# A triangular inverse on TensorE: the second of two matrices is turned on the chip at each level where a product made it before

## The chip, the cores and the metric

One core of one Trainium2 chip runs the whole program in one launch. The metric is the device time of that launch in microseconds (us).

## The reference

Two layers. The first is a recurrent one: for every token of two sequences of 4096 tokens a 512x512 state W and a bias b take one gradient step, and the token's output is read from the new state.

```python
def step(carry, kvq):
    W, b = carry
    k, v, q = kvq
    g = 2.0 / d_h * (W @ k + b - v)
    W = W - LR * jnp.outer(g, k)
    b = b - LR * g
    return ((W, b), W @ q + b)
```

The second is a mixture of experts with one shared expert and the two best of eight for each token. Each layer is followed by a residual sum and a layer norm.

## The kernel before

The recurrence is worked off in 32 steps of 128 tokens (`t` = 0 to 31), both sequences (`b` = 0 and 1) side by side. Within a step, the 128 dependent updates become one unit triangular system of 128x128 for each sequence. Its inverse is needed before the step's updates `U` can be formed (`u_part`), and those before the outputs and the new state.

The inverse is built in four stages. VectorE first inverts the eight diagonal blocks of 16x16 by substitution (`subst`, 30 small instructions). The rows of the blocks reach all partitions by one product with a mask (`spread_blocks`), whose moving operand `R` has 16 x 2 x 16 = 512 columns. Then three levels (`n` = 0, 1, 2) join blocks of 16, 32 and 64. The kernel keeps the matrix `M` (in `MM[:, 0]`) and its transpose (in `MM[:, 1]`). `inv_m` turns the transpose once on TensorE, and ScalarE copies the result to `MM[:, 0]`. A level is: `inv_t`, a product of the system's matrix `LT` with `M`; a masked copy to `T1` on VectorE; `inv_n`, products of `T1` with the transpose; and a subtraction from `MM` on VectorE. On levels 0 and 1, `inv_n` makes two products for each sequence, one for `M` and one for its transpose; on level 2 only the one for the transpose. These products are in plain float32, and each of them stands as two matmul instructions in the trace. All large products of the kernel are instead made of three instructions in float32r (`mm3`, lines 107 to 109), a high part and a low part of each operand.

Each engine follows a list written out by hand. TensorE's puts other work between the dependent parts of the inverse: halves of the next step's key projection (`k_proj`, six matmuls of 512 columns), halves of `qs_part` (six as well), and the shared expert of the step before. That expert's parts are `up_x1`, `back_x1` (two transposes), `down_x1` (six matmuls of 512 columns), once for each sequence. Its hidden tile `Hp1` (`HH` and `HL` in the trace) exists once: ScalarE writes `HH` for sequence 1 only after TensorE's `down_x1` of sequence 0 has read it. In `scalar_program`'s `back_x1` that is

```python
w.wait_ge(k.s_dn1, i)
w.wait_ge(k.s_HS1, i + 1)
copy(k.Hp1[0][:], at["HB", t, b][:, 0:H]).then_inc(k.s_HH1, 1)
```

After the 32 steps the experts of the second layer run over 149 tiles of gathered tokens, up to the end. Two groups of tokens are routed earlier: VectorE does this routing in between its other work, most of it in steps 14 and 26.

Of the kernel before, what the change touches and what calls it, by code (L numbers as in the profile page):

```python
# [15 lines left out]
P = 128  # L16
# [10 lines left out]
LEVELS = [16, 32, 64]  # L27
NL = len(LEVELS)
# [61 lines left out]
def groups_of(NT):  # L90
# [7 lines left out]
    return out, slot  # L98

# [150 lines left out]
def first_memory(k):  # L250

    nc, ctx = k.nc, ExitStack()
    with ctx:
# [30 lines left out]
        k.R = k.MM[:].rearrange("p k b n -> p (k b n)").rearrange("p (i b j) -> p i b j", i=BS, b=NB)  # L284
# [125 lines left out]
def tensor_program(k, e):  # L410
# [86 lines left out]
    def inv_n(t, n):  # L497
# [118 lines left out]
    for t in range(NT):  # L616
# [9 lines left out]
        inv_m(t)  # L626
        if more:
# [31 lines left out]
        else:  # L659
# [106 lines left out]
def scalar_program(k, e):  # L766
# [142 lines left out]
    for t in range(NT):  # L909
# [11 lines left out]
        inv_m(t)  # L921
# [112 lines left out]
def vector_program(k, e):  # L1034
# [39 lines left out]
    def scores(t):  # L1074
# [12 lines left out]
        rows = [P, BS, NB, BS]  # L1087
# [3 lines left out]
        tt(k.R, gd.unsqueeze(1).to_broadcast(rows), unit_lr.unsqueeze(2).unsqueeze(3).to_broadcast(rows), ALU.mult).then_inc(k.s_R, 1)  # L1091
# [944 lines left out]
```

## Time and profile before

| | us |
|---|---|
| median of 3 runs | 2392.36 (2389.82 to 2395.69) |
| the profiled execution, its own time | 2394.0 |
| its span in the trace | 2392.2 |
| TensorE busy with matmuls in the span | 2230.7 |
| VectorE busy | 1534.3 |
| ScalarE busy | 883.9 |

The span is what the trace covers, from the first instruction to the last; 1.8 us of the execution's own time lie around it. Busy times are sums over instructions, and matmuls overlap one another, so a busy TensorE says that it had work and not that it was at its peak. A start-to-start distance of matmuls is what one of them costs in a dense stream.

### The profile page before, as it was taken

What the parts mean: (1) busy time and instruction counts of PE and PEld (TensorE: products, weight loads), DVE (VectorE), ACT (ScalarE), POOL (GpSimd) and SP (SyncE); (2) the same over time, 40 slices, a digit from 0 to 9 for tenths busy, and PEclk for the clock granted to TensorE, in tenths of its full rate; (3) what the DMA queues carried; (4) which work ended last, traced back from release to release, by engine and by line L of the source; (5) the groups of instructions that cost most, each with busy time, mean ns of one, the idle gap of its engine ahead of it and who ended that gap; (6) DMA issues with size and microseconds to landing.
All of it is one profiled execution on the core that took longest, in us unless ns stands there. A gap on an engine that the chain in (4) does not pass through costs nothing.

```text
span 2392.2 us, 40085 instructions
## 1 busy us (share of the span) xinstructions
PE 2230.7 (93%) x13154; PEld 1939.7 (81%) x13154; DVE 1534.3 (64%) x3594; ACT 883.9 (37%) x1887; POOL 1113.8 (47%) x1061
## 2 busy tenths in 40 slices
PE   6999999999999999999999999999869999999860
PEld 5788888888888878888888887888759999989750
DVE  5655666655556667655556667665656545888886
ACT  3333333333333333333333333333346555555420
POOL 1233343433333334644445453356355453777776
PEclk9999999999999999999999999999979999999995
DMA  4011111111111111111111111111264455998996
GB/s 164 18 41 49 36 36 45 45 36 41 49 36 36 36 45 36 45 36 41 49 36 36 45 45 36 36 36 37 93 212 151 152 154 179 307 312 298 298 310 209
DMA packets 102486, 233.26 MB, mean 98 GB/s; under 512 B 18256, under 2 KB 18768, under 8 KB 101520
## 3 DMA queue, kind: packets, MB, share of 16 engines
q1 hardware_dynamic: 75744, 157.96, 18.5%
q0 software_dynamic: 26256, 72.71, 10.5%
q8 instruction: 113, 1.85, 0.3%
q14 instruction: 85, 0.70, 0.1%
q10 hardware_dynamic: 288, 0.04, 0.0%
HBM read 141.11 MB, written 89.53 MB: 96 GB/s over the span
## 4 chain that ended last, share of the span: by engine, by line
PE 82%; DVE 6%; POOL 4%; issue 4%; DMA 3%; ACT 1%; SPq 0%; DVEq 0%; POOLq 0%; ACTq 0%
PE banks L107 23%; PE banks L109 23%; PE banks L108 23%; PE banks L113 7%; POOL RG L1811 2%; PE banks L709 2%; DMA RG<-ys,POS 1%; PE banks L447 1%; PE banks L546 1%; PE banks L731 1%; POOL b_small L1683 1%; DMA ys<-b_Y 1%; POOL b_XN L1799 1%; DVE xc L1055 1%; DVE W L1052 1%
## 5 line engine op out<-in xcount | busy, mean ns | idle before, releaser
L107 PE MATMUL banks<-W 128*128 128x512 f32 (+1 forms) x2040 | 752.9, 369 | 15.9 <-DVE W L1052 15.9
L109 PE MATMUL banks<-W 128*128 128x512 f32 (+1 forms) x2040 | 717.8, 352 | 0.0
L108 PE MATMUL banks<-W 128*128 128x512 f32 (+1 forms) x2040 | 716.6, 351 | 0.0
L107 PEld LDWEIGHTS banks<-W 128*128 128x128 f32 x2040 | 388.5, 190 | 67.7 <-POOL W L1683 15.0
L109 PEld LDWEIGHTS banks<-W 128*128 128x128 f32 x2040 | 387.2, 190 | 54.0
L108 PEld LDWEIGHTS banks<-W 128*128 128x128 f32 x2040 | 388.7, 191 | 50.7 <-issue 7.2
L772 ACT ACTIVATE W<-banks 128x512 fp32r<-128x512 f32 x320 | 191.0, 597 | 521.3 <-DVE banks L1052 243.3
L1683 POOL TENSOR_TENSOR W<-S,W 128x512 fp32r<-128x512 f32 x256 | 327.8, 1306 | 117.3 <-ACT W L772 117.2
L1683 POOL TENSOR_TENSOR X<-X,B 128x1024 f32<-128x1024 f32 x32 | 78.8, 2464 | 620.6 <-DMA X<-in_x 620.6
L772 ACT ACTIVATE W<-S 128x512 fp32r<-128x512 f32 (+1 forms) x288 | 180.4, 650 | 227.8 <-DVE S L1052 211.8
L1052 DVE TENSOR_TENSOR W<-banks,W 128x512 fp32r<-128x512 f32 x192 | 132.2, 688 | 172.3 <-ACT W L772 172.3
L1799 POOL DMA_INDIRECT b_XN<-x1d,IDX x149 | 147.6, 991 | 137.3 <-PE banks L709 107.6
L107 PE MATMUL banks<-W,b_XL 128*128 x596 | 180.9, 304 | 2.0 <-DVE b_XL L1052 1.8
L1055 DVE SCALAR_TENSOR_TENSOR W<-banks,W 128x512 fp32r<-128x512 f32 x128 | 88.6, 692 | 134.1 <-ACT W L772 133.9
L109 PE MATMUL banks<-W,b_XH 128*128 x596 | 168.3, 282 | 0.0
L108 PE MATMUL banks<-W,b_XH 128*128 x596 | 168.0, 282 | 0.0
L1811 POOL DMA_INDIRECT RG<-ys,POS x128 | 139.2, 1087 | 42.2 <-issue 31.4
L1052 DVE TENSOR_TENSOR S<-S,banks 128x512 f32<-128x512 f32 x248 | 156.0, 678 | 0.2 <-issue 0.2
L107 PE MATMUL banks<-W,b_HL 128*128 x298 | 130.7, 439 | 23.0 <-DVE b_HL L1052 22.9
L1730 POOL DMA_INDIRECT ids<-idt,POS x128 | 126.0, 984 | 37.5 <-issue 37.5
L1052 DVE TENSOR_TENSOR b_HL<-banks,b_HH 128x256 fp32r<-128x256 f32 x149 | 62.6, 420 | 110.8 <-ACT b_HH L772 110.8
L772 ACT ACTIVATE b_XH<-banks 128x512 fp32r<-128x512 f32 x149 | 89.1, 598 | 119.3 <-PE banks L709 119.2
(156 smaller groups left out, 4433.6 us busy)
## 6 DMA issues: line engine op xcount, KB each, us to landing
ys<-b_Y SPq DMA_DIRECT2D x149, 256.0 KB
XT<-in_xT SPq DMA_DIRECT2D x32, 512.0 KB, 3.5
X<-in_x SPq DMA_DIRECT2D x32, 512.0 KB, 3.5
x1d<-X SPq DMA_DIRECT2D x64, 256.0 KB, 2.0
zd<-X SPq DMA_DIRECT2D x64, 256.0 KB, 2.0
b_Y<-zd SPq DMA_DIRECT2D x64, 256.0 KB, 5.1
out<-b_Y SPq DMA_DIRECT2D x64, 256.0 KB, 4.4
S<-in_we SPq DMA_DIRECT2D x32, 256.0 KB, 4.6
```

The lines of the kernel that those rows point to most:

```text
L107: e.matmul(o, ll, rh, start=start, stop=False, skip_group_check=True)
L108: e.matmul(o, lh, rl, start=False, stop=False, skip_group_check=True)
L109: return e.matmul(o, lh, rh, start=False, stop=stop, skip_group_check=True)
L113: return e.matmul(o, lhsT, rhs, start=start, stop=stop, skip_group_check=True)
L709: z = e.transpose(o[:, c], k.XN[i % XNS][:, c], ident)
L772: return e.activation(o, i, ACT.Copy, scale=scale)
L1052: return e.tensor_tensor(o, x, y, op)
L1055: return e.scalar_tensor_tensor(out=o, in0=x, scalar=s, in1=y, op0=op0, op1=op1)
L1683: return e.tensor_tensor(o, x, y, op)
L1730: e.indirect_dma_start(k.ids[g["x"]], off, k.idt[:, n:n + 1], None).then_inc(k.d_scatter.sem(m), 16)
L1799: e.indirect_dma_start(k.XN[i % XNS][:], None, k.x1d, off).then_inc(k.d_xs.sem(i), 16)
L1811: e.indirect_dma_start(k.G[j][c % 2], None, k.ys[f.g["x"]], off).then_inc(k.d_gather.sem(m), 16)
```

## The change

On every level the matrix is made by turning its transpose. `inv_m` takes the level `n` as well: TensorE turns `MM[:, 1]` before each of the three `inv_t`, ScalarE copies the result to `MM[:, 0]`, and `inv_t` waits for that copy. `inv_n` makes the product for the transpose alone on all levels, and VectorE's subtraction shrinks from 512 to 256 columns on levels 0 and 1. The order of the lists changes around it. The spread of the blocks leaves out what the substitution never reads: the first 8 rows of a block are sent whole, the last 8 with their last 8 columns only, which makes 8x2x16 + 8x2x8 = 384 columns of 512.

```diff
+HS = BS // 2
+BLK = NB * HS * (BS + HS)
+def block_rows(x):
+    n = NB * HS * BS
+    return [x[:, 0:n].rearrange("p (i b j) -> p i b j", i=HS, b=NB), x[:, n:BLK].rearrange("p (i b j) -> p i b j", i=HS, b=NB)]
 (tensor_program)
     def spread_blocks(t):
-        w.wait_ge(k.s_R, t + 1)
-        mm(e, o, k.cst[:, 2, :], k.R.rearrange("p i b j -> p (i b j)")).then_inc(k.s_Lb, 1)
+        w.wait_ge(k.s_R, 2 * t + 2)
+        mm(e, o[:, 0:BLK], k.cst[:, 2, :], k.R).then_inc(k.s_Lb, 1)
-    def inv_m(t):
-        w.wait_ge(k.s_M, NL * t + 1)
+    def inv_m(t, n):
+        w.wait_ge(k.s_M, NL * t + n + 1)
     def inv_t(t, n):
-        w.wait_ge(k.s_M0, t + 1)
-        w.wait_ge(k.s_M, NL * t + n + 1)
+        w.wait_ge(k.s_M0, NL * t + n + 1)
     def inv_n(t, n):
         for b in range(NB):
-            if not last:
-                mm(e, o[:, b * P:(b + 1) * P], k.MM[:, 1, b, :], k.T1[:, b, :])
-            z = mm(e, o[:, (2 + b) * P:(3 + b) * P], k.T1[:, b, :], k.MM[:, 1, b, :])
+            z = mm(e, o[:, b * P:(b + 1) * P], k.T1[:, b, :], k.MM[:, 1, b, :])
 (the order of a step, TensorE)
             qs_part(t, 0, 0)
-            inv_t(t, 1)
+            inv_m(t, 1)
             if t > 0:
                 down_x1(t - 1, 0)
-            else:
-                qs_part(t, 0, 1)
+            inv_t(t, 1)
+            qs_part(t, 0, 1)
             inv_n(t, 1)
-            if t > 0:
-                qs_part(t, 0, 1)
             k_turn(n, 0)
             k_proj(n, 1, 0)
-            inv_t(t, 2)
+            inv_m(t, 2)
             if t > 0:
                 down_x1(t - 1, 1)
-            else:
-                k_proj(n, 1, 1)
+            inv_t(t, 2)
+            k_proj(n, 1, 1)
             inv_n(t, 2)
-            if t > 0:
-                k_proj(n, 1, 1)
 (the order of the last step, TensorE)
             down_x1(t - 1, 0)
+            inv_m(t, 1)
+            down_x1(t - 1, 1)
             inv_t(t, 1)
-            down_x1(t - 1, 1)
+            qs_part(t, 1, 0)
             inv_n(t, 1)
-            qs_part(t, 1, 0)
+            qs_part(t, 1, 1)
+            inv_m(t, 2)
             inv_t(t, 2)
-            qs_part(t, 1, 1)
             inv_n(t, 2)
 (scalar_program)
-    def inv_m(t):
-        w.wait_ge(k.s_MM, t + 1)
-        w.wait_ge(k.s_T, NL * t)
+    def inv_m(t, n):
+        w.wait_ge(k.s_MM, NL * t + n + 1)
+        w.wait_ge(k.s_T, NL * t + n)
         if t > 0:
             back_x1(t - 1, 1)
+        inv_m(t, 1)
         if more:
             k_turn(n, 0)
             next(soft_steps, None)
+            inv_m(t, 2)
             k_proj(n, 1)
 (vector_program)
-        if n < NL - 1:
-            mmv = k.MM[:].rearrange("p k b n -> p (k b n)")
-            tt(mmv, mmv, o, ALU.subtract).then_inc(k.s_M, 1)
-            return
-        tt(mt, mt, o[:, 256:512], ALU.subtract).then_inc(k.s_MT, 1)
+        tt(mt, mt, o[:, 0:256], ALU.subtract).then_inc(k.s_MT if n == NL - 1 else k.s_M, 1)
             k_proj(n, 0)
-            inv_t(t, 1)
             if t > 0:
                 back_x1(t - 1, 1)
                 down_x1(t - 1, 0)
+            inv_t(t, 1)
             inv_n(t, 1)
             k_turn(n, 0)
-            inv_t(t, 2)
             if t > 0:
                 down_x1(t - 1, 1)
+            inv_t(t, 2)
             inv_n(t, 2)
 (vector_program, scores)
-        tt(k.R, gd.unsqueeze(1).to_broadcast(rows), unit_lr.unsqueeze(2).unsqueeze(3).to_broadcast(rows), ALU.mult).then_inc(k.s_R, 1)
+        for h, o in enumerate(block_rows(k.R)):
+            rows = [P, HS, NB, (BS, HS)[h]]
+            own = unit_lr[:, h * HS:(h + 1) * HS].unsqueeze(2).unsqueeze(3)
+            tt(o, gd[:, :, h * HS:BS].unsqueeze(1).to_broadcast(rows), own.to_broadcast(rows), ALU.mult).then_inc(k.s_R, 1)
```

TensorE, before, in the middle of step 1: level 1 from its first product to its last. `MM,LT` is `inv_t`, `WS,HL` and `WS,HH` are `down_x1` of sequence 0, `T,MM` is `inv_n`'s product for `M` and `MM,T` the one for its transpose. A row is one matmul call.

```order
L113 MATMUL banks<-MM,LT 128x128 [waits s_M,s_LGc]
L113 MATMUL banks<-MM,LT 128x128
L107 MATMUL banks<-WS,HL 128x512
L108 MATMUL banks<-WS,HH 128x512
L109 MATMUL banks<-WS,HH 128x512
L107 MATMUL banks<-WS,HL 128x512
L108 MATMUL banks<-WS,HH 128x512
L109 MATMUL banks<-WS,HH 128x512
L113 MATMUL banks<-T,MM 128x128 [waits s_T1,s_Klo]
L113 MATMUL banks<-MM,T 128x128
L113 MATMUL banks<-T,MM 128x128
L113 MATMUL banks<-MM,T 128x128
```

TensorE, after, the same place; `ident,MM` is the added turn, and the `banks<-W` at the end begin `qs_part`.

```order
L493 MATMUL banks<-ident,MM 128x128 [waits s_M,s_LGc]
L493 MATMUL banks<-ident,MM 128x128
L115 MATMUL banks<-WS,HL 128x512
L116 MATMUL banks<-WS,HH 128x512
L117 MATMUL banks<-WS,HH 128x512
L115 MATMUL banks<-WS,HL 128x512
L116 MATMUL banks<-WS,HH 128x512
L117 MATMUL banks<-WS,HH 128x512
L121 MATMUL banks<-MM,LT 128x128 [waits s_M0,s_Klo]
L121 MATMUL banks<-MM,LT 128x128
L115 MATMUL banks<-W 128x512
L116 MATMUL banks<-W 128x512
```

`inv_t` has moved from ahead of `down_x1` to right behind it, the turn stands where it was, and `inv_t` now waits for `s_M0`, ScalarE's copy.

ScalarE, before, in step 1, from the second activation of the shared expert on (`HH` is its copy for sequence 1):

```order
L851 ACTIVATE banks<-banks,small 128x128 [waits s_hb1]
L851 ACTIVATE banks<-banks,small 128x128
L772 ACTIVATE HH<-banks 128x256 [waits s_HS1,s_dn1]
L772 ACTIVATE W<-banks 128x4x128 [waits s_A,s_Pm,s_KT]
L772 ACTIVATE Kf<-banks 128x512 [waits s_K]
```

ScalarE, after, the same place:

```order
L854 ACTIVATE banks<-banks,small 128x128 [waits s_hb1]
L854 ACTIVATE banks<-banks,small 128x128
L775 ACTIVATE HH<-banks 128x256 [waits s_HS1,s_dn1]
L775 ACTIVATE MM<-banks 128x256 [waits s_T,s_MM]
L775 ACTIVATE W<-banks 128x4x128 [waits s_A,s_Pm,s_KT]
L775 ACTIVATE MM<-banks 128x256 [waits s_T,s_MM]
L775 ACTIVATE Kf<-banks 128x512 [waits s_K]
```

The copy of level 1 stands directly behind the copy to `HH`, which waits for `s_dn1`; the copy of level 2 stands between the copies of the turned and the projected keys.

## Rows read from the trace of the kernel before

**Rows 1.** The page: busy time by engine, and the chain that ended last.

```profile
PE 2230.7 (93%) x13154; PEld 1939.7 (81%) x13154; DVE 1534.3 (64%) x3594; ACT 883.9 (37%) x1887; POOL 1113.8 (47%) x1061
PE 82%; DVE 6%; POOL 4%; issue 4%; DMA 3%; ACT 1%; SPq 0%; DVEq 0%; POOLq 0%; ACTq 0%
```

**Rows 2.** Busy time in stretches: two plain steps, then step 14, which has routing.

```profile
core 0: us, PE busy (x) PEld busy (x) DVE busy (x) ACT busy (x) POOL busy (x), PEclk, DMA share, GB/s
691.00:743.60 52.60, 52.58 (x302) 45.45 (x301) 31.95 (x83) 17.39 (x35) 18.98 (x16) 1.00 0.12 41
744.00:796.00 52.00, 51.98 (x296) 44.88 (x296) 31.39 (x83) 16.92 (x33) 18.98 (x16) 1.00 0.12 41
796.20:856.70 60.50, 54.75 (x303) 46.15 (x302) 43.79 (x106) 21.62 (x39) 20.13 (x16) 0.98 0.10 36
```

**Rows 3.** Timeline of level 1 in step 12: start, duration, engine, instruction.

```profile
696.62 0.40 PE L109 MATMUL banks<-W 128*128 128x512 f32 x1
696.86 0.61 PE L113 MATMUL banks<-MM,LT 128*128 128x128 f32 x4
697.53 0.39 PE L108 MATMUL banks<-WS,HH 128*128 128x512 f32 x1
...
698.46 0.40 PE L109 MATMUL banks<-WS,HH 128*128 128x512 f32 x1
...
698.89 0.39 ACT L772 ACTIVATE HH<-banks 128x256 fp32r<-128x256 f32 x1 [2.62 <-PE banks L109]
...
699.65 0.68 DVE L1052 TENSOR_TENSOR X<-banks,X 128x512 f32<-128x512 f32 x1
699.82 0.39 PE L108 MATMUL banks<-W 128*128 128x512 f32 x1
700.04 0.39 PE L109 MATMUL banks<-W 128*128 128x512 f32 x1
...
700.74 0.40 PE L109 MATMUL banks<-W 128*128 128x512 f32 x1
700.98 0.60 PE L447 MATMUL banks<-ident,Kf 128*128 128x128 f32 x4
701.65 0.39 PE L108 MATMUL banks<-W 128*128 128x512 f32 x1
```

**Rows 4.** Timeline of TensorE around one spread of the blocks (`MM,cst`).

```profile
733.39 1.02 PE L113 MATMUL banks<-MM,cst 128*128 128x512 f32 x2
734.48 0.39 PE L108 MATMUL banks<-W 128*128 128x512 f32 x1
```

**Rows 5.** Instructions of tile HH, and what its engine waited for.

```profile
L772 ACT ACTIVATE HH<-banks x64: 383/385/386, 112.2 to 1758.4; 128x256 fp32r<-128x256 f32 x64
...
  PE banks L109: 81.2, 31
```

**Rows 6.** Timeline of ScalarE at the one copy to `MM` of step 12.

```profile
691.42 0.38 ACT L772 ACTIVATE HF<-banks 128x256 f32<-128x256 f32 x1
691.69 0.39 ACT L772 ACTIVATE MM<-banks 128x256 f32<-128x256 f32 x1
```

**Rows 7.** Timeline of step 0: the one place where `inv_t` waited for that copy.

```profile
55.12 0.38 ACT L772 ACTIVATE MM<-banks 128x256 f32<-128x256 f32 x1
...
55.65 0.68 PE L113 MATMUL banks<-MM,LT 128*128 128x128 f32 x4 [0.30 <-ACT MM L772]
...
56.40 0.40 PE L108 MATMUL banks<-W 128*128 128x512 f32 x1
```

**Rows 8.** Subtraction from `MM`, by shape: total busy us, mean ns.

```profile
L1052 DVE TENSOR_TENSOR MM<-MM,banks 128x512 f32<-128x512 f32 x64 | 43.7, 683 | 58.9 <-PE banks L113 58.9
L1052 DVE TENSOR_TENSOR MM<-MM,banks 128x256 f32<-128x256 f32 x32 | 13.2, 412 | 2.2 <-PE banks L113 2.2
```

**Rows 9.** Stretches with an idle TensorE near step 15; columns as in rows 2.

```profile
843.40:845.90 2.50, 0.35 (x2) 0.00 (x0) 2.50 (x5) 0.54 (x2) 2.50 (x3) 1.00 0.00 0
851.50:854.10 2.60, 0.00 (x0) 0.00 (x0) 2.56 (x12) 0.00 (x0) 0.00 (x0) 1.00 0.00 0
854.40:857.80 3.40, 3.40 (x16) 3.31 (x16) 1.04 (x3) 2.93 (x6) 0.00 (x0) 0.52 0.00 0
908.60:909.90 1.30, 0.02 (x1) 0.05 (x1) 1.30 (x6) 0.00 (x0) 0.00 (x0) 1.00 0.00 0
```

More of the change, by code:

```diff
@@ L283, in first_memory @@
         k.onesr, k.cst = sb("onesr", [P], F32R), sb("cst", [NCST, P])
-        k.R = k.MM[:].rearrange("p k b n -> p (k b n)").rearrange("p (i b j) -> p i b j", i=BS, b=NB)
+        k.R = k.MM[:].rearrange("p k b n -> p (k b n)")[:, 0:BLK]
         k.xc, k.rw = sb("xc", [NB, BS]), sb("rw", [KC, E])
@@ L476, in spread_blocks @@
         o = bank(w, ("Lb", t), k.s_sub, 2 * (BS - 1) * (t + 1))
-        w.wait_ge(k.s_R, t + 1)
-        mm(e, o, k.cst[:, 2, :], k.R.rearrange("p i b j -> p (i b j)")).then_inc(k.s_Lb, 1)
-    def inv_m(t):
-        o = bank(w, ("MM", t), k.s_M0, t + 1)
-        w.wait_ge(k.s_M, NL * t + 1)
+        w.wait_ge(k.s_R, 2 * t + 2)
+        mm(e, o[:, 0:BLK], k.cst[:, 2, :], k.R).then_inc(k.s_Lb, 1)
+    def inv_m(t, n):
+        o = bank(w, ("MM", t, n), k.s_M0, NL * t + n + 1)
+        w.wait_ge(k.s_M, NL * t + n + 1)
         for b in range(NB):
@@ L625, in tensor_program @@
             up_x1(t - 1, 1)
-        inv_m(t)
+        inv_m(t, 0)
         if more:
@@ L808, in scores @@
         copy(k.ATp[0][:], kq).then_inc(k.s_AThi, 1)
-    def inv_m(t):
-        w.wait_ge(k.s_MM, t + 1)
-        w.wait_ge(k.s_T, NL * t)
-        copy(k.MM[:, 0, :, :].rearrange("p b n -> p (b n)"), at["MM", t][:, 0:256]).then_inc(k.s_M0, 1)
+    def inv_m(t, n):
+        w.wait_ge(k.s_MM, NL * t + n + 1)
+        w.wait_ge(k.s_T, NL * t + n)
+        copy(k.MM[:, 0, :, :].rearrange("p b n -> p (b n)"), at["MM", t, n][:, 0:256]).then_inc(k.s_M0, 1)
     def inv_end(t):
@@ L920, in scalar_program @@
             up_x1(t - 1, 1)
-        inv_m(t)
+        inv_m(t, 0)
         if more:
@@ L935, in scalar_program @@
                 split_w(m)
+            inv_m(t, 2)
         inv_end(t)
@@ L1086, in scores @@
         e.tensor_reduce(gd, k.T1[:].rearrange("p b (k j) -> p b j k", k=NBL), AX.X, ALU.add).then_inc(k.s_sc, 1)
-        rows = [P, BS, NB, BS]
         w.wait_ge(k.s_sc, 4 * t + 3)
@@ L1090, in scores @@
         w.wait_ge(k.s_MTlo, t)
-        tt(k.R, gd.unsqueeze(1).to_broadcast(rows), unit_lr.unsqueeze(2).unsqueeze(3).to_broadcast(rows), ALU.mult).then_inc(k.s_R, 1)
-        w.wait_ge(k.s_R, t + 1)
+        for h, o in enumerate(block_rows(k.R)):
+            rows = [P, HS, NB, (BS, HS)[h]]
+            own = unit_lr[:, h * HS:(h + 1) * HS].unsqueeze(2).unsqueeze(3)
+            tt(o, gd[:, :, h * HS:BS].unsqueeze(1).to_broadcast(rows), own.to_broadcast(rows), ALU.mult).then_inc(k.s_R, 1)
+        w.wait_ge(k.s_R, 2 * t + 2)
         stt(kq, kq, -1.0, mAT.unsqueeze(1).to_broadcast(bc), ALU.add, ALU.mult).then_inc(k.s_sc, 1)
@@ L1099, in subst @@
     def subst(t):
-        n0, lb = 2 * (BS - 1) * t, at["Lb", t].rearrange("p (i b j) -> p i b j", i=BS, b=NB)
+        n0, (upper, lower) = 2 * (BS - 1) * t, block_rows(at["Lb", t])
         w.wait_ge(k.s_Lb, t + 1)
@@ L1105, in subst @@
         for b in range(NB):
-            stt(k.xc[:, b, 1:BS], lb[:, 0, b, 1:BS], unit[:, 0:1], unit[:, 1:BS], ALU.mult, ALU.add).then_inc(k.s_sub, 1)
+            stt(k.xc[:, b, 1:BS], upper[:, 0, b, 1:BS], unit[:, 0:1], unit[:, 1:BS], ALU.mult, ALU.add).then_inc(k.s_sub, 1)
         yield
@@ L1111, in subst @@
                 w.wait_ge(k.s_sub, n0 + 2 * j + b - 1)
-                stt(rest, lb[:, j, b, j + 1:BS], k.xc[:, b, j:j + 1], rest, ALU.mult, ALU.add).then_inc(k.s_sub, 1)
+                row = upper[:, j, b, j + 1:BS] if j < HS else lower[:, j - HS, b, j + 1 - HS:HS]
+                stt(rest, row, k.xc[:, b, j:j + 1], rest, ALU.mult, ALU.add).then_inc(k.s_sub, 1)
             yield
@@ L1488, in vector_program @@
             tick()
-            inv_t(t, 1)
-            tick()
             if t > 0:
@@ L1495, in vector_program @@
                 tick()
+            inv_t(t, 1)
+            tick()
             inv_n(t, 1)
@@ L1499, in vector_program @@
             tick()
-            inv_t(t, 2)
-            tick()
             if t > 0:
@@ L1504, in vector_program @@
                 tick()
+            inv_t(t, 2)
+            tick()
             inv_n(t, 2)
@@ L1519, in vector_program @@
             down_x1(t - 1, 0)
-            inv_t(t, 1)
             split_w(1)
             down_x1(t - 1, 1)
+            inv_t(t, 1)
             inv_n(t, 1)
@@ L1525, in vector_program @@
             inv_t(t, 2)
+            inv_n(t, 2)
             split_w(4)
-            inv_n(t, 2)
             split_w(6)
```

## The prediction

> **What bounds the kernel now.** I read the page first: TensorE is busy for 2230.7 us of 2392.2, and the chain that ended last runs on it for 82% [rows 1]. Then the stretches, since an average mixes 32 steps with the experts behind them. In a plain step TensorE is busy 52.58 of 52.60 us, at full granted clock, with VectorE at 31.95 and ScalarE at 17.39 us [rows 2]. So in these steps every matmul taken away is time taken away, and every wait of TensorE's is time added, in full: there is no idle time in the step for a new wait to hide in. Steps 14 and 26 (60.50 us for the first of them [rows 2]) have some on TensorE, where VectorE's routing is late. Last I read one step's timeline for what a matmul costs in the stream [rows 3] and for what ScalarE is doing when it will be wanted [rows 3, 5].
>
> **What the change removes.** Take the distance from a 512-column matmul, over a small group and one L107, to the next L108. Over `inv_t`'s four instructions it is 697.53 - 696.62 = 0.91 us; over `inv_n`'s eight it is 699.82 - 698.46 = 1.36 us [rows 3]. The difference, 0.45 us, is four instructions, which is exactly what a level loses. Levels 0 and 1 each lose it: 0.90 us a step.
>
> **What it adds on TensorE.** Four transposes, two each ahead of levels 1 and 2. The group of four key transposes takes 701.65 - 700.74 = 0.91 us by the same measure [rows 3]; two 512-column matmuls are in it, at 0.23 each (four of them from 699.82 to 700.74), so four transposes cost 0.91 - 0.46 = 0.45 us, the price of two products. A transpose is one instruction where a product is two, and they cost the same each. Bounds: 0.42 to 0.46.
>
> **The spread.** From its start to the next L108 are 734.48 - 733.39 = 1.09 us, 0.23 of which is the L107 between: 0.86 us for 512 columns [rows 4]. With 384 columns three quarters: 0.215 us less. TensorE is dense there, so it counts. If a fixed part does not shrink, it is a little less; lower bound 0.15.
>
> So TensorE's own work shrinks by 0.90 - 0.45 + 0.215 = **0.665 us a step**, 20.6 us over steps 0 to 30.
>
> The Trainium skill ("Perfetto Trace Analysis", Transposes) asks that a logical transpose be made by the transpose and not by a standard matmul, and gives as its reason that arithmetic is skipped. By that rule the change is right as it stands; the rows agree only on the count of instructions, since one transpose instruction costs the 0.11 us that one pass of a product costs.
>
> **What it adds as a wait.** `inv_t` of a level now waits for ScalarE's copy to `MM`. What is queued ahead of that copy on ScalarE decides. On level 0 nothing changes. On level 1 the copy stands directly behind `back_x1` of sequence 1, whose last instruction, the copy to `HH`, waits for `down_x1` of sequence 0. The trace shows this wait in every step: ScalarE idles 2.62 us and starts 0.43 us after the start of `down_x1`'s last matmul [rows 3], 31 times [rows 5]. It hurt nobody. But in the new order TensorE runs turn, `down_x1` of sequence 0, `inv_t`. So `down_x1`, meant as the cover for the copy, is what the copy waits for, through the ScalarE queue: the cover is gone entirely. Counted from the start of that last matmul:
>
> - `HH` starts at 0.43;
> - the next ScalarE instruction starts 0.27 later, as 691.42 to 691.69 for a copy of the same size followed by this very copy [rows 6]: 0.70;
> - the copy to `MM` takes 0.39 [rows 6]: 1.09;
> - TensorE starts `inv_t` 0.15 after the copy's end (55.12 + 0.38 to 55.65), and from there to the next L108 are 56.40 - 55.65 = 0.75 [rows 7]: 1.99.
>
> Without a wait the same distance is 0.91 [rows 3], 0.23 of it for the first matmul; the restart alone costs 0.75 - 0.68 = 0.07. The wait costs **1.08 us**, in each of steps 1 to 30. Bounds: 0.9 if part of the restart is an artefact of modelled matmul ends; 1.3 if the copy's reads and ScalarE's waits add one more handover of 0.15 to 0.2.
>
> Who else is late? VectorE's masked copy to `T1` on level 1 now stands behind `HL` and the residual sum of `down_x1`. The sum starts at 1.19 after my zero and takes 0.68 [rows 3]; `inv_t` ends near 1.24 + 0.68 = 1.92, so `T1` is done near 2.4, and `inv_n` comes at 1.24 + 0.44 + 6 x 0.23 = 3.06. Covered by 0.6 us. On level 2 the copy is behind the copy of the turned keys, whose transposes are a half `k_proj` (1.4 us) older, and a whole `down_x1` of 1.4 us lies between turn and `inv_t`, against 0.04 + 0.39 + 0.15 = 0.58 of need. Covered. In step 14 the routing's exponential sits between, still covered by my count, by about 0.1 us.
>
> **The ends.** In step 0 there is no shared expert, so on levels 1 and 2 `inv_t` follows its turn at once. A group of four transposes lasts 0.60 and its last starts at 3 x 0.11 [rows 3], so the last ends 0.27 after its start; 0.04 + 0.39 + 0.15 bring `inv_t` to 0.85 instead of 0.11, and the restart costs 0.07 more: 0.8 us each, 1.6 together, less 0.665. That is +0.9. In the last step level 2 has nothing between turn, `inv_t` and `inv_n`: two bare handovers of about 0.8, less 0.665, less 0.27 for level 0's subtraction, for which level 1 waits there and which takes 412 ns in place of 683 [rows 8]. I take +0.7 (0 to 2). In steps 14 and 26 TensorE waits for VectorE near the step's end anyway (2.5 us with 0.35 busy [rows 9]), so the spread's 0.215 is not gained there: +0.4. The first spread, in the prologue, is on the way: -0.2.
>
> **Sum.** 30 x (1.08 - 0.665) = +12.5; +0.9 + 0.7 + 0.4 - 0.2 = +1.8. Together +14.3 us. Against the profiled execution's own 2394.0 that is 2408.3; that execution stands 1.6 above the median of the runs, 2392.4, from which the forecast is 2406.7, say **2406.5 us**. A difference of 0.3%, 7.2 us, is about what a measurement of this kernel can tell from no change.
>
> **Rivals.**
>
> *The copy is hidden* (7%). If ScalarE's copy to `MM` did not have to stand behind `HH`, or `HH` were released early, only the savings stay: -20.6 + 1.8 = -18.8, or 2373.6 us. This is the case on the other side; it decides as soon as the wait costs less than 0.665 us a step. Against it stands the 2.62 us idle of ScalarE in [rows 3] and the order of its instructions.
>
> The Trainium skill ("PSUM — Partial Sum Buffer", Engine vs sequencer instructions) says that ScalarE's queue is strictly first in, first out, while TensorE may pull a weight load ahead but keeps its matmuls in order. By that rule nothing overtakes `HH`, and the forecast stands; the 2.62 us of idle agree, for the copy of the turned keys behind it had nothing to do with `down_x1`.
>
> *The wait is there but smaller* (5%). With 0.6 to 0.9 us a step the result lies between -0.2 and +9: 2392 to 2401, mostly within 0.3%. For it: the ends of matmuls are modelled. Against it: `HH` starts at a fixed 0.43 us behind, so the real end is where it is modelled.
>
> *The clock falls* (4%). After 2.60 us of an idle TensorE the granted clock was 0.52 for 3.40 us [rows 9], the lower level of 1.2 GHz in place of 2.4; at half speed such a stretch loses 1.7 us. If each new wait brought that, 30 x 1.7 = 51 us come on top: 2458. Against it: after 1.3 us idle at 908.6, longer than the new wait, and during the 2.5 us at 843.4 the clock stayed at 1.00 [rows 9].
>
> The Trainium skill ("TensorE: Matmul & The Clock Gate", Part 4: PE-mode transpose) says that transposes do not count as work for the clock, which would favour this rival since the change adds some. No row here shows it: plain steps, which hold such groups as the one at 700.98 [rows 3], run at 1.00 [rows 2].
>
> *VectorE becomes the one waited for* (within the forecast's range). If the 0.6 us of cover for `T1` were gone, each step would lose up to 0.3 us more, 9 us in all: 2416.
>
> **How the numbers follow.** The forecast has 84%. Its own spread comes from 0.9 to 1.3 us for the wait (-5 to +7), the spread product (2 us), the ends (1 us) and the runs' own scatter (3 us); the two low terms rarely meet, so I give 2400 to 2413 for eight in ten. Slower by over 0.3%: 0.88, which takes in the clock's rival and the forecast. Faster: 0.07. Within: 0.05.
>
> **What would show it.** In a plain step of the changed kernel: `inv_t` of level 1 with an idle time ahead of it near 0.8 us, put down to ScalarE's `MM`; `HH` still with its 2.6 us idle, and an `MM` copy 0.27 us behind it; no idle ahead of `inv_t` of level 2; plain steps longer by 0.4 us, each with eight instructions of the `inv_n` kind gone and four transposes come. Wrong if the copy on ScalarE starts before `HH`, if TensorE waits at another place, or if the clock in the plain steps is under 1.00.

## The result, and the profile after

The changed kernel takes 2415.41 us, the median of 4 runs (2412.13 to 2419.0), against 2392.69 for the kernel before beside it: 1.0092 times as long [1.008, 1.0104], 22.7 us more. The forecast was 2406.5 us with a range of 2400 to 2413, so the sign is right and the size is not. The profiled execution took 2416.47 us, span 2414.7.

The page of the changed kernel, busy time by engine (compare [rows 1]):

```profile
PE 2225.8 (92%) x13026; PEld 1927.7 (80%) x13026; DVE 1526.3 (63%) x3626; ACT 901.8 (37%) x1951; POOL 1113.5 (46%) x1061
```

TensorE is busy for 4.9 us less, with 128 instructions fewer, and yet the span is 22.5 us longer: the change saved work and added waiting. (The busy time is a sum over overlapping rows and holds the half-clock stretches; what was saved in a step is measured below.) Where, is asked of the waits first. The two largest of TensorE's waits between step 1 and the last step, in the changed kernel (engine, line, releaser; total us, times, longest):

```profile
PE banks L121 <- ACT MM L775: 27.3, 32, 1.1
PE banks L115 <- DVE X1l L1058: 12.0, 6, 2.7
```

The same question to the kernel before:

```profile
PE banks L107 <- DVE X1l L1052: 12.5, 6, 2.7
PE banks L113 <- ACT MM L772: 1.1, 1, 1.1
```

The waits for `X1l` stand still, 12.5 us before and 12.0 after. Those for `MM` have gone from one to 32, from 1.1 to 27.3 us. Thirty of them are level 1 of steps 1 to 30, 0.84 us each; the other two are at level 0, in steps 1 and 27. `L121` is `inv_t`'s product, `ACT MM` the copy of the turned matrix. One of these waits, level 1 of step 12, in the timeline of the changed kernel (start, duration, engine, instruction; in brackets the idle time before it and what ended it); it answers to [rows 3]:

```profile
700.93 0.38 PE L493 MATMUL banks<-ident,MM 128*128 128x128 f32 x2
...
702.30 0.40 PE L117 MATMUL banks<-WS,HH 128*128 128x512 f32 x1
702.74 0.38 ACT L775 ACTIVATE HH<-banks 128x256 fp32r<-128x256 f32 x1 [2.09 <-PE banks L117]
703.02 0.38 ACT L775 ACTIVATE MM<-banks 128x256 f32<-128x256 f32 x1
703.15 0.42 DVE L1058 TENSOR_TENSOR HL<-banks,HH 128x256 fp32r<-128x256 f32 x1 [2.26 <-ACT HH L775]
703.50 0.68 DVE L1058 TENSOR_TENSOR X<-banks,X 128x512 f32<-128x512 f32 x1
...
703.54 0.68 PE L121 MATMUL banks<-MM,LT 128*128 128x128 f32 x4 [0.84 <-ACT MM L775]
...
704.29 0.39 PE L116 MATMUL banks<-W 128*128 128x512 f32 x1
```

Read from the top. `down_x1`'s last matmul starts at 702.30. ScalarE, idle for 2.09 us (the prediction's sign said 2.6), is released by it and copies `HH` at 702.74. Only then, 0.28 us later, does it copy `MM`, whose transposes, at 700.93, were done long before. TensorE stands idle for 0.84 us and restarts at 703.54. From 702.30 to the next L116 at 704.29 are 1.99 us, the figure that the prediction had added up. A whole plain step, from its first turn to the next one's (columns as in [rows 2]):

```profile
695.40:748.50 53.10, 52.24 (x298) 44.95 (x297) 31.60 (x84) 18.02 (x37) 19.02 (x16) 1.00 0.12 41
```

53.10 us, where the kernel before has 52.65 by the same measure (the starts of the first `ident,MM` of one step and the next; most plain steps repeat it within 0.05). The granted clock stays at 1.00, its upper level, so the idle 0.84 us costs no clock. The spread and the turns, by shape, in the changed kernel (total us, mean ns of one, idle before):

```profile
L493 PE MATMUL banks<-ident,MM 128*128 128x128 f32 x192 | 36.7, 272 | 3.8 <-DVE MM L1058 3.8
...
L121 PE MATMUL banks<-MM,cst 128*128 128x384 f32 x64 | 26.1, 488 | 0.3 <-DVE S L1058 0.2
```

Stage by stage, in the two profiled executions. Each stage is bounded by starts on TensorE: the first turn of a step, the first matmul of `u_part` in the last step, the first transpose of the experts.

| stage | before, us | after, us | difference | forecast |
|---|---|---|---|---|
| prologue, to step 0's first turn | 53.5 | 51.9 | -1.6 | -0.2 |
| step 0 | 56.91 | 58.17 | +1.3 | +0.9 |
| steps 1 to 30 | 1600.0 | 1613.7 | +13.7 | +12.9 |
| last step, to `u_part` | 15.92 | 20.51 | **+4.6** | +0.7 |
| `u_part` to the experts | 38.30 | 38.83 | +0.5 | 0 |
| experts | 627.5 | 631.5 | +4.1 | 0 |

Steps 1 to 30 came out as forecast. The last step did not, and neither did the experts, which are looked at further down. The first two rows can't be read from one pair of traces: the prologue of the kernel before took 51.8 us in its later trace and 53.5 here, and step 0 varies with the clock. Step 0 of the changed kernel took 58.17 us at a mean granted clock of 0.91 and 55.67 at 1.00 (`after_again` below, the same program); at 0.94 the changed levels took 57.64 (`hh_again` below) and the old ones 56.9 and 57.2 (the two traces of the kernel before), which makes +0.4 to +0.7.

The end of the last step in the changed kernel, where the inverse's result `MTl` is due at TensorE:

```profile
1738.99 0.42 DVE L1058 TENSOR_TENSOR MM<-MM,banks 128x256 f32<-128x256 f32 x1 [0.80 <-PE banks L121]
1739.33 3.43 DVE L1058 TENSOR_TENSOR W<-S,W 128x512 fp32r<-128x512 f32 x2
1739.34 2.86 POOL L1688 TENSOR_TENSOR X<-X,B 128x1024 f32<-128x1024 f32 x1 [18.73 <-DMA X<-in_x]
...
1742.17 3.12 POOL L1688 TENSOR_TENSOR W<-S,W 128x512 fp32r<-128x512 f32 x2
1742.68 1.48 DVE L1058 TENSOR_TENSOR MTl<-MM,MTh 128x256 fp32r<-128x256 f32 x1
...
1744.30 0.77 PE L115 MATMUL banks<-W,MTl 128*128 128x512 f32 x1 [5.36 <-DVE MTl L1058]
```

The same place in the kernel before:

```profile
1724.84 0.42 DVE L1052 TENSOR_TENSOR MM<-MM,banks 128x256 f32<-128x256 f32 x1 [0.81 <-PE banks L113]
1725.18 0.68 DVE L1052 TENSOR_TENSOR W<-S,W 128x512 fp32r<-128x512 f32 x1
...
1725.81 0.43 DVE L1052 TENSOR_TENSOR MTl<-MM,MTh 128x256 fp32r<-128x256 f32 x1
...
1726.38 0.47 PE L107 MATMUL banks<-W,MTl 128*128 128x512 f32 x1 [1.58 <-DVE MTl L1052]
...
1726.67 2.41 POOL L1683 TENSOR_TENSOR X<-X,B 128x1024 f32<-128x1024 f32 x1 [19.36 <-DMA X<-in_x]
```

Before, between `MM` and `MTl` on VectorE stands one split of an expert weight (`W<-S,W`), 0.68 us, and TensorE waits 1.58 us. Only after `MTl` does GpSimd start its 128x1024 sum `X<-X,B`. In the changed kernel two splits stand there, for the change also moves `inv_n` of level 2 in VectorE's list for the last step, a part of the edit that the excerpt of the change does not show:

```diff
 (vector_program, the order of the last step)
             inv_t(t, 2)
+            inv_n(t, 2)
             split_w(4)
-            inv_n(t, 2)
             split_w(6)
             inv_end(t)
```

The two splits take 3.43 us in place of two times 0.68: one by one 0.68 and 2.83. `MTl` takes 1.48 in place of 0.43. TensorE waits 5.36 us. All the while GpSimd is at work: on that sum, which starts within 0.01 us of the splits, and from 1742.17 on splits of its own. That is two theories at once: the order of the list (O), and a VectorE that slows beside GpSimd (G).

### The profile page after: what moved, and what is told of

Its sections match the earlier page's. It is cut to its first block, busy times and chain, and to the rows that moved or that the text cites. A ratio compares the mean times of both kernels' runs of the same rounds, so it can differ in the third digit from the quotient of the medians.

```text
span 2414.7 us, 39989 instructions
## 1 busy us (share of the span) xinstructions
PE 2225.8 (92%) x13026; PEld 1927.7 (80%) x13026; DVE 1526.3 (63%) x3626; ACT 901.8 (37%) x1951; POOL 1113.5 (46%) x1061
## 4 chain that ended last, share of the span: by engine, by line
PE 81%; DVE 6%; issue 4%; POOL 4%; DMA 3%; ACT 1%; SPq 0%; DVEq 0%; POOLq 0%; ACTq 0%
PE banks L115 23%; PE banks L117 23%; PE banks L116 23%; PE banks L121 6%; PE banks L712 2%; POOL RG L1816 2%; DMA RG<-ys,POS 2%; PE banks L455 1%; PE banks L551 1%; PE banks L734 1%; PE banks L493 1%; DVE xc L1061 1%; POOL b_small L1688 1%; POOL b_XN L1804 1%; DVE W L1058 1%
## 5 line engine op out<-in xcount | busy, mean ns | idle before, releaser
L116 PE MATMUL banks<-W 128*128 128x512 f32 (+1 forms) x2040 | 717.3, 352 | 0.0
L116 PEld LDWEIGHTS banks<-W 128*128 128x128 f32 x2040 | 388.8, 191 | 46.5
L116 PE MATMUL banks<-W,b_XH 128*128 x596 | 169.4, 284 | 0.0
```

The costliest lines, as they stand in the source:

```text
L116: e.matmul(o, lh, rl, start=False, stop=False, skip_group_check=True)
```

## The experiments

The first four kernels below shared their runs of the kernel before, 2393.35 us (20 runs), which agrees with the 2392.69 of the result, so that they are compared with the changed kernel's 2415.41 too. In the later sessions every version, the kernel before included, took some 40 us longer, so that ratios are taken within a session only; what that was is looked at behind the last experiment. HH stands for the theory that `HH` ahead of the copy on ScalarE costs the step 1.08 us, O and G for the two above.

**Copy `MM` first.** The changed kernel, with ScalarE's copy for level 1 ahead of the copy to `HH`, in steps 1 to 30.

```diff
 (ScalarE, the copy to HH, sequence b of step t)
+        if b == 1 and t + 2 < NT:
+            inv_m(t + 1, 1)
         w.wait_ge(k.s_dn1, i)
         ...
         copy(k.Hp1[0][:], at["HB", t, b][:, 0:H]).then_inc(k.s_HH1, 1)
 (ScalarE, the order of a step)
             back_x1(t - 1, 1)
-        inv_m(t, 1)
+        if t == 0 or not more:
+            inv_m(t, 1)
```

> The changed kernel, with one move on ScalarE in steps 1 to 30: the copy to MM of level 1 stands ahead of the copy to HH (which waits for down_x1 of sequence 0), and no longer behind it. Theory A (the copy was late because it was queued behind HH): the idle time of 0.84 us ahead of inv_t of level 1 goes, a plain step falls from 53.10 us by 1.08 to 52.02, and the whole by 30 x 1.08 = 32.4 us, to about 2383 us, some 9.5 us under the kernel before. Rival B (the wait is the bare way from turn to copy to inv_t, and the queue has nothing to do with it): the step stays at 53.1 and the time at 2415 us. In between: what is left of the idle is the part that the queue does not explain.

Measured: 2390.13 us (10 runs), 0.9992 [0.9982, 1.0002] of the kernel before, and 25 us less than the changed kernel. The plain step is 52.31, not 52.02. So HH is right that the wait hangs on the queue, and 0.28 us a step remain. Level 1 of step 11 in this kernel:

```profile
637.85 0.39 ACT L775 ACTIVATE MM<-banks 128x256 f32<-128x256 f32 x1 [0.69 <-PE banks L493]
...
639.04 0.60 PE L121 MATMUL banks<-MM,LT 128*128 128x128 f32 x4
639.24 0.38 ACT L775 ACTIVATE HH<-banks 128x256 fp32r<-128x256 f32 x1 [1.01 <-PE banks L117]
...
639.65 0.42 DVE L1061 TENSOR_TENSOR HL<-banks,HH 128x256 fp32r<-128x256 f32 x1 [2.26 <-ACT HH L775]
...
640.00 0.68 DVE L1061 TENSOR_TENSOR X<-banks,X 128x512 f32<-128x512 f32 x1
...
640.59 0.41 DVE L1061 TENSOR_TENSOR T<-banks,smallc 128x256 f32<-128x256 f32 x1
640.64 0.40 PE L117 MATMUL banks<-W 128*128 128x512 f32 x1
...
641.06 0.52 PEld L121 LDWEIGHTS banks<-MM,T 128*128 128x128 f32 x4 [0.46 <-DVE T L1061]
641.06 0.71 PE L121 MATMUL banks<-MM,T 128*128 128x128 f32 x4
```

`MM` is now copied at 637.85 and `inv_t` starts at 639.04 with no wait. But `HH` still waits for `down_x1`, VectorE's `HL` and residual sum `X` for `HH`, and the masked copy to `T1` (`T<-banks`) stands behind both, at 640.59. `inv_n` waits for it: its weight load says 0.46 us. The row of the matmul itself shows no wait, because the modelled end of the matmul at 640.64 covers it; in a dense stream the next one would have started 0.23 behind, at 640.87, and it starts at 641.06, 0.19 late; its four instructions then take 0.71 us in place of 0.61. The two make the 0.28 us, within rounding. The prediction had given `T1` 0.6 us of cover. That cover was there only because `inv_t`, and `inv_n` behind it, were themselves 1.08 us late.

**A second buffer for `HH`.** The changed kernel; sequence 1's `HH` gets a tile of its own, so that its copy no longer waits for `down_x1` of sequence 0.

```diff
+        k.HH1s = [k.Hp1[0], sb("HH1b", [H], F32R)]
 (ScalarE)
-        w.wait_ge(k.s_dn1, i)
+        w.wait_ge(k.s_dn1, i - 1)
-        copy(k.Hp1[0][:], at["HB", t, b][:, 0:H]).then_inc(k.s_HH1, 1)
+        copy(k.HH1s[b][:], at["HB", t, b][:, 0:H]).then_inc(k.s_HH1, 1)
 (TensorE's down_x1 and VectorE's back_x1)
-        hi, lo = k.Hp1
+        hi, lo = k.HH1s[b], k.Hp1[1]
```

> The changed kernel with its lists as they are, and a second buffer for HH of sequence 1, so that this copy no longer waits for down_x1 of sequence 0. HL keeps its one buffer. Theory A: ScalarE's queue is free, the copy to MM follows the turn at once, the idle ahead of inv_t of level 1 goes, plain steps of about 52.02 us, the whole about 2383 us (-32), as with the copy moved ahead. Rival B: 2415 us, as nothing that stands between turn and inv_t has changed but the wait of another instruction. Rival C (it is the order of the lists, not the wait on the buffer, that costs): a remainder of 0.3 us or more per step.

Measured: 2380.29 us (4 runs), 0.9944 [0.9929, 0.9959]. The plain step is 52.03. TensorE's waits for `MM` between step 1 and the last step, in this kernel (both are at level 0), and then its level 1 of step 12:

```profile
PE banks L121 <- ACT MM L776: 1.8, 2, 0.9
```

```profile
686.45 0.38 ACT L776 ACTIVATE HH1b<-banks 128x256 fp32r<-128x256 f32 x1
...
687.04 0.38 ACT L776 ACTIVATE MM<-banks 128x256 f32<-128x256 f32 x1 [0.21 <-PE banks L494]
...
688.24 0.61 PE L121 MATMUL banks<-MM,LT 128*128 128x128 f32 x4
688.51 0.42 DVE L1059 TENSOR_TENSOR HL<-banks,HH1b 128x256 fp32r<-128x256 f32 x1 [1.91 <-PE banks L117]
...
689.45 0.41 DVE L1059 TENSOR_TENSOR T<-banks,smallc 128x256 f32<-128x256 f32 x1
...
690.08 0.61 PE L121 MATMUL banks<-MM,T 128*128 128x128 f32 x4
```

The `MM` copy follows its turn at 687.04, 1.2 us before `inv_t` starts, and `T1` is 0.2 us early instead of late. Only in steps 16 and 28 does TensorE wait for `T1` (0.55 and 0.42 us). 53.10 - 52.03 = 1.07 us a step is the price of the wait; the forecast said 1.08. With the queue released the change is worth having.

**The spread alone.** The kernel before, with the 384-column spread and nothing of the inverse.

```diff
+HS = BS // 2
+BLK = NB * HS * (BS + HS)
-        w.wait_ge(k.s_R, t + 1)
-        mm(e, o, k.cst[:, 2, :], k.R.rearrange("p i b j -> p (i b j)")).then_inc(k.s_Lb, 1)
+        w.wait_ge(k.s_R, 2 * t + 2)
+        mm(e, o[:, 0:BLK], k.cst[:, 2, :], k.R).then_inc(k.s_Lb, 1)
 (VectorE: k.R written in two parts, the rows of a block read from them, as in the change)
```

> The kernel before with the narrow spread alone (384 columns of 512, and its two VectorE instructions). Theory A's sum has 0.215 us a step for it: plain steps of 52.65 - 0.215 = 52.43 us, 31 x 0.215 = 6.7 us in all, 2386 us. Rival F (the two instructions on VectorE or the substitution behind them take it back, since VectorE had only 0.54 us to spare before the sum with B): plain steps between 52.5 and 52.65, and no difference that can be measured.

Measured: 2386.72 us (10 runs), 0.9972 [0.9962, 0.9981]; plain step 52.44. The spread gives 0.21 us a step, as forecast (0.215). What is left between 52.44 and 52.03 is the levels' own part: 0.41 us, where the forecast had 0.45.

**The splits behind `MTl`.** The changed kernel; in the last step VectorE makes `MTl` before the two splits. This takes theory O alone.

```diff
             inv_n(t, 2)
+            inv_end(t)
             split_w(4)
             split_w(6)
-            inv_end(t)
             split_w(7)
```

> The changed kernel with one move on VectorE in the last step alone: the low parts of weights 4 and 6 are made behind the low part of the inverse (MTl), not ahead of it. In the changed kernel they stood ahead of it for 3.4 us and TensorE idled 5.36 us before u_part. Theory D (this queue is the part that my sum of the ends left out): the idle before u_part falls to about 1.6 us, u_part comes 3.8 us earlier, and the time falls to about 2411.6 us. Rival E (the weights' transfers set the end of that phase anyway): u_part comes earlier, but the first expert tile at the same time as before, and the time stays at 2415 us.

Measured: 2411.35 us (4 runs), 1.0077 [1.0062, 1.0093]: 4.1 less than the changed kernel. The last step up to `u_part` is 18.25 us in place of 20.51, with TensorE still idle for 3.10, not 1.6:

```profile
1737.53 2.34 POOL L1688 TENSOR_TENSOR X<-X,B 128x1024 f32<-128x1024 f32 x1 [18.66 <-DMA X<-in_x]
...
1738.21 1.94 DVE L1058 TENSOR_TENSOR MTl<-MM,MTh 128x256 fp32r<-128x256 f32 x1 [0.55 <-ACT MTh L775]
...
1740.30 0.77 PE L115 MATMUL banks<-W,MTl 128*128 128x512 f32 x1 [3.10 <-DVE MTl L1058]
```

Nothing but `MTl` itself is left on VectorE here, and it takes 1.94 us for what takes 0.43 elsewhere. GpSimd's sum runs from 1737.53 to 1739.87. Moving the splits gives back 2.3 us, and what remains looks like G.

**GpSimd later.** To hold G against O, the changed kernel with its two splits ahead of `MTl`, but GpSimd's sum of the last step held back until `MTl` is made.

```diff
 (GpSimd)
         w.wait_ge(k.s_B, 2 * t)
+        if t == NT - 1:
+            w.wait_ge(k.s_MTlo, NT)
         tt(k.X[:], k.X[:], k.B[:], ALU.add).then_inc(k.s_XB, 1)
```

> The changed kernel with one more wait on GpSimd in the last step: its sum X + B starts only when VectorE has finished the low part of the inverse (MTl). Lists and work are the same. In the changed kernel this sum ran from 1739.34 to 1742.20 us, and two splits of weights and MTl on VectorE, which took 0.68, 0.68 and 0.43 us where GpSimd was idle, took 3.43 us for the two and 1.48 us in that stretch; with the splits moved behind, MTl took 1.94 us instead. Theory G (VectorE is slowed by GpSimd's large operation at the same time, and this is most of what the last step lost): the two splits and MTl take about 1.8 us together, the idle before u_part falls from 5.36 to about 2.2 us, the time by 3.2 us to about 2412 us. Rival H (the VectorE instructions are late or long for another reason, such as the transfers that land then): they stay long and the time stays at 2415 us.

Measured: 2454.79 us (7 runs) against 2436.69 for the kernel before beside it, in the second session, and the step up to `u_part` is 17.29 us. The changed kernel was not timed beside these two. The ratio, 1.0068 [1.0049, 1.0087], stands against its 1.0092 [1.008, 1.0104] in the first and 1.0097 [1.0075, 1.012] in the third; the intervals overlap, and the trace decides:

```profile
1759.38 1.29 DVE L1058 TENSOR_TENSOR W<-S,W 128x512 fp32r<-128x512 f32 x2
...
1760.58 0.42 DVE L1058 TENSOR_TENSOR MTl<-MM,MTh 128x256 fp32r<-128x256 f32 x1
...
1761.15 0.47 PE L115 MATMUL banks<-W,MTl 128*128 128x512 f32 x1 [2.14 <-DVE MTl L1058]
1761.17 2.67 POOL L1688 TENSOR_TENSOR X<-X,B 128x1024 f32<-128x1024 f32 x1 [20.47 <-DVE MTl L1058]
```

The same two splits take 1.29 us in place of 3.43, and `MTl` 0.42 in place of 1.48, with the same instructions, order and operands; only GpSimd is silent. That is 2.14 + 1.06 = 3.2 us, and the stage is 20.51 - 17.29 = 3.2 shorter. G is shown. The 2.14 us that TensorE still waits are 0.56 more than the 1.58 before: the second split, which is O by itself.

The rows say more than "slower". In `split_last` the sum ends at 1739.87 and `MTl` at 1740.15, 0.28 us behind it. Over the fourteen traces of this case, each of the 11 `MTl` that start while GpSimd is in such a sum or split ends 0.28 or 0.29 us behind GpSimd's end, and each of VectorE's 105 splits of 128x512 that do so ends 0.54 to 0.56 us behind, whether it lasts 1.03 us or 2.87. So VectorE's instruction waits until GpSimd's is done. The other way round it is GpSimd that gives way: in the changed kernel VectorE's first split starts 0.01 us ahead of the sum and takes its usual 0.68 us, and the sum takes 2.86 us where it took 2.34 in `split_last`. Work with an operand in PSUM does not wait. Two rows of the kernel before, from where GpSimd is in its sum and then in a split:

```profile
1727.99 1.40 DVE L1055 SCALAR_TENSOR_TENSOR W<-banks,W 128x512 fp32r<-128x512 f32 x2 [1.15 <-ACT W L772]
1729.31 1.57 DVE L1052 TENSOR_TENSOR W<-S,W 128x512 fp32r<-128x512 f32 x1
```

The two of the first row take 0.69 us each, as anywhere; the one of the second, with both operands in SBUF, takes 1.57 in place of 0.68.

**Both mends.** The second buffer and the splits behind `MTl` (`hh_and_split`), and with GpSimd held as well (`all_three`); the edits are the ones above.

> The changed kernel with the second buffer for HH and with the two splits of the last step moved behind MTl. If the two causes add up: 2380.3 (second buffer alone) less 2.3 us (what u_part gained in the trace with the splits moved, 20.51 to 18.25 us from the step's first turn) to less 4.1 us (what the whole gained): 2376 to 2378 us. Rival: the last step's gain is lost in the loading of weights behind it, 2380 us.

> The changed kernel with the second buffer for HH, the splits moved behind MTl and GpSimd's sum X + B held back until MTl is done. Theory G: MTl takes 0.43 us and not 1.9, u_part comes 16.6 to 17 us after the last step's first turn (15.9 before the change, 20.5 after it, 18.3 with the splits moved alone), and the time is 1 to 2 us under the run without the wait on GpSimd: 2375 to 2377 us, or 0.7% under the kernel before. Rival: holding GpSimd back delays the sum that o_part needs and gives it back, no difference to the run without it.

Measured: 2427.03 us (10 runs), 0.9964 [0.9946, 0.9982], and 2429.97 us (12 runs), 0.9968 [0.9955, 0.9981]. Holding GpSimd brings the stage before `u_part` from 17.81 to 16.39 us, but the whole gets nothing. The last step of `all_three`:

```profile
1731.05 5.13 DVE L1059 TENSOR_TENSOR W<-S,W 128x512 fp32r<-128x512 f32 x3
...
1731.31 2.66 POOL L1689 TENSOR_TENSOR X<-X,B 128x1024 f32<-128x1024 f32 x1 [19.60 <-DVE MTl L1059]
...
1736.84 0.50 PE L115 MATMUL banks<-W,ATl 128*128 128x512 f32 x1 [2.66 <-DVE W L1062]
```

The collision has only moved: now three splits meet GpSimd's sum and its own splits and take 5.13 us, and TensorE waits 2.66 us for VectorE at `ATl`. From `u_part` to the experts it is 40.63 us, where `hh_and_split` has 39.70.

**The same again, against each other.** A third session, with the changed kernel, the second buffer, both mends, and all three.

> The changed kernel itself once more, beside the three versions below on one chip. The last three runs were on another chip, where the kernel before took 2436.7 us in place of 2393.4 and the steps with scatters were longer in all versions, so their differences to runs of the first chip can't be read. Expected: 1.009 times the kernel before; in steps 1 to 13 53.10 us each; from the last step's first turn to u_part 20 to 21 us.

> The second buffer for HH alone, as in second_hh. Expected 0.9944 of the kernel before, steps 1 to 13 52.03 us, and 20 to 21 us from the last step's first turn to u_part.

> The second buffer for HH and the splits of the last step behind MTl. On the other chip 0.9964 of the kernel before there, 17.8 us from the last step's first turn to u_part. If the causes add up: 2.5 to 4 us under the second buffer alone, 0.9930 of the kernel before. If the loading of the weights behind the last step sets the time: no difference to the second buffer alone.

> The same and GpSimd's sum X + B held back until MTl is done. On the other chip u_part came 16.4 us after the last step's first turn, MTl took 0.43 us, but the next low part of u_part came late, behind three splits of weights that now met GpSimd's sum for 5.13 us. Theory G with that: u_part 1.4 us earlier than in the run before this one, o_part not earlier, and no difference in time between the two, within 2 us.

| kernel | us | ratio to before [95%] | plain step | last step, to `u_part` |
|---|---|---|---|---|
| changed | 2458.63 | 1.0097 [1.0075, 1.012] | 53.10 | 21.60 |
| second buffer | 2425.78 | 0.9972 [0.9961, 0.9984] | 52.00 | 20.92 |
| and splits behind `MTl` | 2421.42 | 0.9956 [0.994, 0.9972] | 52.00 | 17.75 |
| and GpSimd held | 2420.72 | 0.9949 [0.9934, 0.9964] | 52.00 | 16.41 |

The changed kernel's ratio repeats (1.0092, 1.0097). The last two rows can't be told apart. Both mends together beat the kernel before by 0.4%, and by their medians they are 4.4 us below the second buffer alone; the intervals of these two just overlap.

**What differs between the sessions.** The kernel before, unchanged, once more.

> The kernel before once more, for its trace in a session in which it takes about 2435 us and not 2393. If the session or chip costs every version the same: plain steps 1 to 13 of 52.65 us as in the first trace, steps 18 to 25 longer by 0.6 to 1 us each, the last two steps of the recurrence and the expert phase longer by 8 to 10 and by 20 to 25 us. If this chip is as fast as the first, the trace repeats the first one and says nothing on that.

Measured: 2435.14 us (8 runs), 1.0001 [0.9981, 1.0022] of itself. Its plain steps outside a few are 52.65, as in the first session. Longer are steps 18 to 25 (53.25 to 53.49), steps 29 and 30 (59.51 and 61.35), and the experts (648.0 in place of 627.5). So the extra 40 us lie in a few steps (20) and in the experts (20), and the plain steps and `u_part`'s stage (15.93) can be compared over all sessions. It weakens the comparison of whole times: the two mends' 0.4% holds in that condition; in the first session only the second buffer alone was timed, and was 0.56% faster, where the third gave it 0.28%. That it was another chip, as some of the expectations say, is not shown: the first and the third session are on record under the same chip number.

## Why the prediction was right in part

**Right, row for row: the wait at level 1.** `HH` behind `down_x1`, the copy 0.28 us behind `HH`, TensorE's restart, 1.99 us in all. Taking the queue's wait away brought 1.07 us a step (forecast 1.08). The spread brought 0.21 (0.215), the levels 0.41 (0.45). A plain step got 0.45 us longer (forecast 0.415). The wait and the spread are each shown by a run in which it alone was changed; the levels' part is what is left over.

ScalarE's copies come strictly in the order of the list: the `MM` copy's transposes start at 700.93 and end by 701.31 in the changed kernel's trace, and the copy starts at 703.02, behind `HH`. The Trainium skill ("PSUM — Partial Sum Buffer", Engine vs sequencer instructions) gives that as the rule, and by that rule the forecast of the sign held.

**Right in sum, not in place: steps 14, 15, 26, 27.** The forecast had 1.2 us for 14 and 26 together and 0.8 for 15 and 27. The traces give -0.07, +1.27, +0.05, +0.77, 2.0 us together as well. The shift between the two steps of a pair is one of the clock. Behind one of TensorE's idle times in a routing step (2.4 to 2.75 us) the granted clock is at its lower level for 3.4 us. In the kernel before, that stretch lies mostly in step 14 ([rows 9], 854.40 to 857.80; step 14 ends at 856.67). In the changed kernel it lies mostly in step 15, which begins at 861.99:

```profile
861.40:864.70 3.30, 3.30 (x12) 2.82 (x12) 1.20 (x3) 2.78 (x6) 0.00 (x0) 0.50 0.00 0
```

By half of the 1.5 us that changed sides, step 14 is shorter and step 15 longer by some 0.75 us (an estimate). In steps 26 and 27 it has moved the other way, and there TensorE's second wait for VectorE is 1.45 us in place of 2.74. So the sum of 2.0 is right by some luck.

**The step that failed: "In the last step level 2 has nothing between turn, `inv_t` and `inv_n` ... I take +0.7 (0 to 2)".** It was +4.6. The part that this sentence costed, the bare handovers, is about right. With the splits and GpSimd out of the way the stage is 16.4 us; 0.35 us of that is a gain of the second buffer, which these versions have too (TensorE waits 1.00 us ahead of level 1's turn, and 1.35 without the buffer). That leaves 16.75 against 15.92, +0.8. What the sentence left out is who else is on VectorE. The change also moves `inv_n` of level 2 ahead of `split_w(4)` in VectorE's list, so two splits stand between the last subtraction and `MTl`, where one stood. With GpSimd held back that costs 17.29 - 16.75 = 0.5 us, the 0.56 seen above. And that lands the splits and `MTl` beside GpSimd's sum and splits. The sum began 0.4 us behind `MTl`'s end before; the overlap costs 3.2 us. Together 0.8 + 0.5 + 3.2 = 4.5 of the 4.6 us. I had read the edit as a matter of TensorE's order, and counted only TensorE's instructions and ScalarE's copy in it. This step alone does not carry the time out of the range: with +4.6 in its place the sum gives 2410.6 us. The other 4 to 5 us are mostly the experts, which the sum had at nothing.

**A smaller miss: the 0.6 us of cover for `T1`.** It was right as a number and wrong as a reserve. It would have been gone as soon as the wait ahead of it was, and `copy_first` ran into that: the rival "The copy is hidden" priced at 2373.6 was 2390.13 for the one version and 2380.29 for the other. In the second, 0.04 us a step, the last step's 4.3 (20.93 - 15.92 - 0.7) and 1.6 for steps 16 and 28, which wait for `T1`, account for the 6.7 us that are missing.

**What is not explained.** Of the 22.5 us between the two spans the stages up to the experts give 18.4. The other 4.1 are the experts', whose code the change doesn't touch. Over the first session's traces this stage takes 627.5 and 625.8 us in the two versions with the old levels (the kernel before and `spread_only`) and 628.9 to 631.5 in the four with the changed ones, so a part of it may come from the change after all; by one trace each that is not shown. The changed kernel's trace has half-clock stretches in it where the kernel before has none, as here (columns as in [rows 2]):

```profile
1790.00:1793.40 3.40, 3.40 (x19) 3.40 (x18) 0.00 (x0) 0.90 (x2) 1.58 (x3) 0.53 0.72 212
```

They don't settle it: over the stage the mean granted clock is 0.94 before and 0.93 in the changed kernel, and 0.93 too in `spread_only`, the shortest of all. Why they come and go is open.

**The rivals.** "The clock falls" is refuted: 30 idle stretches of 0.84 us, and the granted clock is 1.00 in the plain steps. It fell behind a longer one: during the last step's idle 5.36 us it went to 0.50, and `u_part`'s first matmul takes 0.77 us in place of 0.47. "VectorE becomes the one waited for" is refuted for the changed kernel as it is, where `T1` appears among the waits only in the last step (0.52 us, one of the bare handovers), and true of `copy_first`. That this rival's 2416 us is so near the 2415.41 measured is chance; it also lay outside the range that it was said to be within.

## What to carry to other kernels

When a value now goes round by another engine, look at what is queued ahead of it there, and what *that* waits for. A cover that consists of the very work the queue waits for is none. Reorder the queue or, better, give the instruction ahead of it a buffer of its own: moving the copy left the next victim one step behind, and the buffer cured both in the plain steps.

Read a change of order on every engine's list, the last iteration's own list too. Ask of each engine what then runs at the same time: a slack found while another wait is in place is not a reserve, and a VectorE time taken beside a silent GpSimd doesn't hold beside a busy one. What it costs is the rest of GpSimd's instruction, so look for the longest one.

## What the runs showed of the hardware

- A VectorE subtraction of two SBUF tiles that starts while GpSimd is in its fp32 sum of 128x1024 or a split of 128x512 ends 0.28 us (128x256) or 0.55 us (128x512) behind GpSimd's instruction: up to 1.94 us in place of 0.42, and up to 2.87 in place of 0.68. With one operand in PSUM it takes its usual 0.69. The Trainium skill ("Perfetto Trace Analysis", Optimizing Scalar/DVE Operations) says that the two share an SBUF port; this case's rows agree, and put the price at the time that GpSimd's instruction has left. Whether it is that port was not tried by itself.
- An fp32 transpose of 128 columns costs TensorE what one of a product's two instructions costs, about 0.11 us: eight product instructions fewer and four transposes more saved 0.41 us a step, where equal prices give 0.45. The turns' mean in the rows above is 272 ns, modelled end included, against 275 and 282 for the products' instructions.
- A matmul's row can hide up to 0.17 us of a wait behind the modelled end of the one before it (0.40 us long, where the next may start after 0.23). The weight load's row shows it.
- In the longer sessions ScalarE, and more rarely VectorE, stand idle in some steps until something that the trace calls remote: some 4.5 us in steps 18 to 22 of the kernel before, once 10.8 on ScalarE, up to 7.6 on VectorE over all versions. One row of the kernel before, in its last run:

```profile
1020.38 0.60 ACT L772 ACTIVATE Kf<-banks 128x512 f32<-128x512 f32 x1 [4.48 <-remote]
```

  None of the six traces of the first session has a row of that kind. The cause is open.
